# Waits among POOL's 32 scatters in the first attention: from the last eight to the eight before them, on two semaphores

## What is computed

```python
# layer 0
xn = layernorm(x)
s = window_attention(xn)            # 16 heads, windows of 64, softmax with a relative bias
top1 = argmax(xn @ w_router)        # one of 32 experts for every row
slot = where(pos < 160, top1 * 160 + pos, nowhere)
buf = zeros(32 * 160, 256).at[slot].set(xn)     # the scatter
y = (silu(buf @ w_gate) * (buf @ w_up)) @ w_down
x = x + s * silu(xn + gate * y[slot])
# layer 1
xn = layernorm(x)
s = unbind(cumsum(bind(unit(K), unit(V))), unit(Q))    # by Fourier transforms
f = top-2 of 8 experts, hidden width 1024
x = x + s * silu(f)
```

## Time and profile before

| | |
|---|---|
| median of 3 runs | 1120.48 us (1119.7 to 1121.26) |
| the profiled execution's own time | 1118.83 us |
| its span on the core | 1116.9 us |
| PE busy | 1029.4 us, 92% |
| DVE busy | 688.7 us, 62% |
| ACT busy | 533.3 us, 48% |
| POOL busy | 418.5 us, 37% |
| mean granted clock of TensorE | 0.966 of full speed |

### The profile page before, as it was taken

The page is one execution under the profiler, slowest core; times in us unless marked ns, Lnnn a source line. Parts: engine busy times, 40 slices in busy tenths (PEclk is TensorE's granted clock), DMA queues, the critical chain, the costliest instruction groups (busy, mean ns, idle before and its releaser), DMA issues.

```text
span 1116.9 us, 16806 instructions
## 1 busy us (share of the span) xinstructions
PE 1029.4 (92%) x6152; PEld 887.9 (79%) x6152; DVE 688.7 (62%) x1490; ACT 533.3 (48%) x1102; POOL 418.5 (37%) x391
## 2 busy tenths in 40 slices
PE   3867899999999994988999999999999999999995
PEld 2655688888888873678889998988888888888884
DVE  6777777777777767688855644474766200048853
ACT  4634654555455536743444545455453233256531
POOL 1046544554545452200243322332331345522363
PEclk9879999999999996987999999999999999999998
DMA  9932236445555428525487854544344679989971
GB/s 307 280 134 86 85 112 185 156 165 180 161 182 187 142 88 264 196 85 240 121 321 261 280 203 182 202 172 187 109 134 188 221 267 348 332 302 388 390 283 64
DMA packets 120402, 228.65 MB, mean 205 GB/s; under 512 B 14939, under 2 KB 103915, under 8 KB 115329
## 3 DMA queue, kind: packets, MB, share of 16 engines
q1 hardware_dynamic: 106448, 189.31, 48.9%
q0 software_dynamic: 13872, 38.27, 10.3%
HBM read 166.98 MB, written 62.79 MB: 206 GB/s over the span
## 4 chain that ended last, share of the span: by engine, by line
PE 74%; DVE 11%; ACT 5%; issue 3%; DMA 3%; POOL 2%; SPq 1%; POOLq 0%; DVEq 0%; ACTq 0%
PE PS L1321 21%; PE PS L1331 20%; PE PS L1220 6%; PE PS L1055 5%; PE PS L1105 3%; PE PS L1159 2%; PE PS L1230 2%; PE PS L1186 2%; POOL table L2342 2%; PE PS L1114 2%; PE PS L1197 2%; PE PS L1172 2%; PE PS L1307 1%; PE PS L1296 1%; DVE hot_tile L1846 1%
## 5 line engine op out<-in xcount | busy, mean ns | idle before, releaser
L2299 ACT ACTIVATE hT<-PS,WE 128x256 f32<-128x256 f32 (+1 forms) x312 | 141.5, 455 | 255.1 <-PE PS L1321 251.8
L1321 PE MATMUL PS<-xgT,WE 128*128 128x256 f32 (+1 forms) x1248 | 253.0, 361 | 1.4 <-ACT xgT L2286 0.7
L1331 PE MATMUL PS<-WE,hT 128*128 128x256 f32 x1104 | 244.6, 379 | 0.0
L1321 PEld LDWEIGHTS PS<-xgT,WE 128*128 128x128 f32 x1248 | 219.4, 190 | 28.0 <-ACT xgT L2286 0.9
L1331 PEld LDWEIGHTS PS<-WE,hT 128*128 128x128 f32 x1104 | 207.4, 190 | 27.0
L1958 DVE TENSOR_TENSOR y<-PS,WE 128x512 f32<-128x512 f32 (+1 forms) x38 | 24.3, 640 | 205.7 <-PE PS L1331 205.7
L2417 POOL DMA_INDIRECT result<-y,result_of x53 | 53.7, 1014 | 173.7 <-DVE y L1958 166.4
L2405 POOL DMA_INDIRECT xg<-xn_dram,token_of x71 | 74.5, 1049 | 91.5 <-DVE result_of L1874 69.1
L1055 PE MATMUL PS<-XT,Wf 128*128 128x256 f32 x384 | 96.1, 407 | 3.3 <-ACT Z L2076 3.3
L1055 PEld LDWEIGHTS PS<-XT,Wf 128*128 128x128 f32 x384 | 76.7, 205 | 15.9 <-ACT Z L2076 4.9
L2358 POOL TENSOR_TENSOR prob<-prob,row_sum 128x512 f32<-128x512 f32 x56 | 58.7, 1047 | 59.8 <-DVE row_sum L1538 59.5
(11 more groups left out here) (280 smaller groups left out, 1722.1 us busy)
## 6 DMA issues: line engine op xcount, KB each, us to landing
WE<-in_experts SPq DMA_DIRECT2D x39, 2180.0 KB, 9.3
wgu<-in_w_gate SPq DMA_DIRECT2D x32, 256.0 KB, 2.8
wgu<-in_w_up SPq DMA_DIRECT2D x32, 256.0 KB, 3.1
wdn<-in_w_down SPq DMA_DIRECT2D x32, 256.0 KB, 3.7
result<-zeros SPq DMA_DIRECT2D x16, 512.0 KB, 4.8
xs<-late_dram SPq DMA_DIRECT2D x16, 512.0 KB, 13.6
both<-result SPq DMA_DIRECT2D x16, 512.0 KB, 8.3
table<-zeros POOLq DMA_DIRECT2D x1, 5160.0 KB, 31.4
```

What stands on the lines that cost most here:

```text
L1321: m = e.matmul(PS[:, FIRST_H_BANK + nth % HR, 0:rows], W1[n % WR][:, k, c * P:(c + 1) * P], xgT[:, n % 2, k, 0:rows], start=k == 0, stop=k ...
L1331: m = e.matmul(PS[:, u.bank, j * D:(j + 1) * D], hT[:, n % 2, c, j * P:(j + 1) * P], W2[n % WR][:, c, :], start=c == 0, stop=c == KF - 1)
L2299: e.activation(hT[:, n % 2, c, 0:rows], PS[:, FIRST_H_BANK + (KF * n + c) % HR, 0:rows], ACT.Gelu_apprx_tanh, bias=b1[n % WR][:, c:c + 1], ...
```

## The change

The single semaphore of the scatters becomes two, `scattered[0]` and `scattered[1]`. Issues 0 to 7 and 16 to 23 add to the first, issues 8 to 15 and 24 to 31 to the second. Ahead of issue 8 nothing is waited for. Ahead of issue 16 POOL waits for 128 on the first (issues 0 to 7 landed), ahead of issue 24 for 128 on the second (issues 8 to 15 landed). SP waits for both to reach 256 ahead of its first load from the table. The writes of `late_put` add to the second, in place of `late_stored`, and the last wait of POOL counts from 16 * 16 on.

```diff
@@ signals
-    scattered0 = signal("scattered0")
+    scattered = [signal("scattered_even"), signal("scattered_odd")]
-    late_step, late_ready, late_stored = signal("late_step"), signal("late_ready"), signal("late_stored")
+    late_step, late_ready = signal("late_step"), signal("late_ready")
@@ gpsimd, route0_put
                 for t in range(NT):
-                    if t % 8 == 0:
-                        w.wait_ge(scattered0, 16 * t)
+                    if t % 8 == 0 and t > 8:
+                        w.wait_ge(scattered[t // 8 % 2], 16 * 8 * (t // 16))
                     e.indirect_dma_start(
                         out=table0, out_offset=bass.IndirectOffsetOnAxis(ap=slot_put[:, t:t + 1], axis=0),
-                        in_=XN[:, t, :], in_offset=None, bounds_check=SLOTS0 - 1, oob_is_err=False).then_inc(scattered0, 16)
+                        in_=XN[:, t, :], in_offset=None, bounds_check=SLOTS0 - 1, oob_is_err=False).then_inc(
+                            scattered[t // 8 % 2], 16)
@@ gpsimd, late_put and last
-                in_offset=None, bounds_check=T - 1, oob_is_err=False).then_inc(late_stored, 16)
+                in_offset=None, bounds_check=T - 1, oob_is_err=False).then_inc(scattered[1], 16)
-                w.wait_ge(late_stored, 16 * LATE_TILES)
+                w.wait_ge(scattered[1], 16 * (NT // 2 + LATE_TILES))
@@ sync, load0_first
-                w.wait_ge(scattered0, 16 * NT)
+                for i in range(2):
+                    w.wait_ge(scattered[i], 16 * NT // 2)
```

## The result

| | before | changed |
|---|---|---|
| median | 1121.26 us (1119.7 to 1121.96, 5 runs) | 1146.4 us (1144.65 to 1148.68, 5 runs) |
| profiled execution, span | 1118.83, 1116.9 us | 1148.68, 1146.7 us |
| mean granted clock | 0.966 | 0.95 |

The ratio is 1.0223, with a 95% interval of 1.0206 to 1.024. The prediction said 1118.1, so it was wrong, and by far.

A forecast was written before the change was run, and what follows sets the result against it. The prediction took PE, busy 92%, as the bound: 5.9 us off POOL's waits, less some 0.5, put the subtractions 5.4 earlier, of which 2.4 count: 1120.48 - 2.4 = 1118.1 us; 8-in-10 range 1115.8 to 1120.5.

The forecast's parts named there:

- Step 1, the three waits: POOL's scatter issues: three gaps of about 2.27 us shrink to 0.30 each, saving 5.9 us.
- I cost both at nothing: The two waits left, ahead of issues 16 and 24, never stop POOL, since earlier scatters have landed; cost nothing.
- whatever the waits allow: On POOL at most four scatters can be under way at once (4.3 / 1.27), regardless of the waits.
- Step 2, the long scatters: Scatters meeting DVE operations: about seven in place of five, some 0.5 us more; POOL's first subtraction at 107.15, 5.4 earlier.
- The Trainium skill's rule of the shared interface: A DVE instruction with two SBUF inputs and a GpSimd instruction reading SBUF share an interface; the later one blocks.
- Step 3, 2.4 us: Attention start to the scores behind K's copy: PE's Q products stay at 111.46, scores come 2.3 to 2.5 us earlier.
- the product with V without idle time: Sign on PE: the product with V runs at 113.4 without idle time.
- if PE's Q products move: Sign against the central step: PE's Q products, expected still at 111.46, would start at another time.
- Step 4, what carries it on: From those scores to the end PE's work is all but closed, so the 2.4 us move on unchanged.
- The slower one: Rival: PE's clock comes back one 5 us stretch later at layer 1's start, +2.6 us net, 1123.1; chance 0.05.

The follow-up runs named there:

- e10_again: The changed kernel run again, nothing edited: median 1114.64 us, ratio 0.9963 to before, no stall in ten runs.
- e3_fours: Changed kernel with the two semaphores taking groups of four in turns, POOL waiting for the group before the last: 1116.33 us, ratio 0.9977.
- e2_two_strict: Changed kernel, two semaphores kept, but POOL waits for the last eight ahead of issues 8, 16 and 24: 1118.47 us, ratio 1.0003.
- e4_sixes: As e3_fours, with groups of six in place of four: 1115.89 us, ratio 0.9976.
- e5_fives: As e3_fours, with groups of five in place of four: 1115.24 us, ratio 0.9981.
- e11: Changed kernel with its two semaphores renamed, all else alike: 1151.31 us, ratio 1.0244.
- e12_no_waits: Changed kernel with semaphores renamed and no wait among the 32 scatter issues: 1151.21 us, ratio 1.0249.
- e13: The changed kernel again, nothing edited, as yardstick: 1148.51 us, ratio 1.0233.
- e15: Same kernel as e4_sixes, nothing edited, run beside a stall: 1150.91 us, ratio 1.0253.
- e16: The changed kernel again, nothing edited, as yardstick: 1151.53 us, ratio 1.0213.
- e19_pauses: Changed kernel plus 16 small scratch memsets on POOL ahead of issues 8, 16 and 24: 1148.69 us, ratio 1.018.
- e6: As e3_fours, with groups of seven in place of four: 1115.61 us, ratio 0.9974.
- e9: Changed kernel, but POOL waits ahead of issue 8 for the first eight and ahead of issue 24 for issues 8 to 15: 1116.53 us, ratio 0.9983.
- e17_before: The kernel before the change, nothing edited, traced beside a stall of the changed kernel: 1125.44 us, ratio 0.9993.
- e18_two_strict: Same kernel as e2_two_strict, nothing edited, run beside a stall of the changed kernel: 1127.05 us, ratio 1.0001.

## Why the prediction was wrong

*Step 1, the three waits.* Right on POOL itself: no landing was waited for, and 31 gaps of 0.30 us were left. **This is the step that failed:** its sum "6.8 - 3 x 0.30 = 5.9 us" costed the waits only by what they take from POOL, and took the three stops for pure loss, and its "I cost both at nothing" asked of the two waits that are left only whether they stop POOL. What taking the stops away does to other engines was put at nothing without a reason. In the measurement of the change the stops were worth some 25 us (1146.4 - 1121.26), by one wait of 32.37 us on DVE for finished work of PE. The count of scatters under way, "whatever the waits allow", was beside the point: where the disturbance is there, it is not how many are under way, but whether POOL's stream has its stops. The forecast's own trace held a stretch of 10 us and then a stop, three times over, and no stretch of 41 us; whether such a stretch is harmless was an extrapolation that I didn't mark as one.

*Step 2, the long scatters.* First subtraction 107.15 by the forecast, 107.13 in e10_again. Part of that is luck: the first scatter starts 0.38 us earlier there (64.23 for 64.61), so POOL's way to the subtraction was 0.4 us longer than forecast. There are 8 scatters over 1.05 us, where seven were expected and before had 5. Beside the stall only one is long, since DVE stands. The Trainium skill's rule of the shared interface ("SBUF — State Buffer", Who interferes with whom) fits this, though nothing here tested it alone.

*Step 3, 2.4 us.* Right in its mechanism where the stall is away: 10.78 - 8.36 = 2.4 in e10_again, the product with V without idle time, and 1.51 us of waiting ahead of the scores, where 1.3 was forecast. Between DVE's marks the eight loosened kernels without a stall (e3 to e10) need 76.7 to 79.0 us, the kernel before and e2_two_strict 80.0 and 80.4. Their ratios of 0.9963 to 0.9983 hold the forecast's 0.9979; e10_again gains more than 2.4 us, since PE's products of Q stand 1.3 us earlier in its trace (110.18 for 111.46) and the step took them for fixed. By the prediction's own sign ("if PE's Q products move") that is a miss: 0.4 of it is the earlier start of the scatters, the other 0.9 stands behind it (46.85 us from the first scatter to these products before, 45.95 in e10_again and e3_fours, but 46.9 again in e4_sixes and e5_fives), and what moves them wasn't followed.

*Step 4, what carries it on.* Right in both cases: behind the scatters nothing is given back. With the stall DVE's 241st instruction is 29.4 us later than before, and the span's end 29.8.

*The rivals.* The slower one counted on PE's clock. The clock was down here, 0.61 from 64 to 110 us, in a stretch in which PE was busy 11.47 of 46 us: it went with PE's standing, which the semaphore updates explain. No rival had a semaphore update that is late in itself. The rows of before gave no sign of it: the stops are 2.3 us each, about what a landing takes (2.4 to 2.5), and the updates of PE are on time in that trace. What could have been noted is that no row shows POOL scattering for over 10 us at a time.

## What stays open

Four measurements showed the stall for every kernel without stops (the first one, e11 with e12, e13 to e15, e16 with e19), and three showed it for none (e2 to e5, e6 to e9, e10). What differs between them isn't known: not the program, not a chip as such. Medians of the kernel before lean the same way, 1118.02, 1118.67 and 1120.09 us where there was no stall, 1121.26, 1124.74, 1121.42 and 1126.02 where there was. The trace of before that the forecast read (1118.83 us, all its records) lies below all five runs that stood beside the change (1119.7 to 1121.96), so it may have been taken without the disturbance that they had; no trace of theirs is kept. In the stalled kernels the copy of K starts 4.1 to 4.6 us behind the end of the last scatter (106.88 to 111.02 in the first), where in the stops it took 1.1 to 1.6; that isn't explained either, nor is why two of the late updates of the first trace (87.89, 94.92) came while POOL was scattering. e19_pauses doesn't follow this, with its K already copied at 94.09. Not tried: stops after every four scatters, which might cut the 1 to 4 us by which updates are late in the kernel before, and other work of POOL long enough to split the stream.

No version beat both: the loosened kernels are 0.2 to 0.4% faster without the disturbance and 1.8 to 2.5% slower with it. The kernel before, with its three stops, is the one to keep.

## What to carry to other kernels

A wait that seems only to cost time may limit how long an engine goes on without a break, and another engine may need that break. Before taking it out, look for the longest stretch that the trace shows without such a stop, and count everything beyond it as untested; here it was 10 us, and the change made it 41. And measure a gain of 0.2% in more than one measurement, since the same file gave 0.9963 and 1.0233: when an experiment doesn't reproduce a stall, run the stalled kernel itself beside it before drawing anything from it.

## What was new about the hardware

- TensorE's semaphore updates can arrive 13 to 34 us after its products while POOL issues indirect DMAs of 128 rows of 1032 bytes without a stop (32 in 41 us), and 1 to 4 us late when it stands for 2.3 us after every eighth (e17_before, e18_two_strict). In other measurements of the same file they are on time.
- The updates' own records grow thin with it (100 of the scatters' 512 landings in the changed kernel, 198 in e17_before), from the first scatter on. In the traces here missing landings and late updates go together, even in a kernel that hardly loses time by them.
- POOL's sequencer hands over up to 12 indirect DMAs that the engine has not begun (13 in e12_no_waits).
